# Two window-attention blocks rewritten: 32-row score products, strips of windows, other engine orders and longer loops

## The chip, the cores and the metric

The kernel runs on one core of a Trainium2 chip. The metric is device time in microseconds, the median of the runs. The engines are PE (matmul; its weight loads are listed as PEld), DVE (vector), ACT (scalar, activation tables), POOL (GpSimd) and SP, whose queue issues the DMAs. SBUF is the on-chip memory, PSUM the eight accumulator banks (512 float32 in each of 128 partitions) that PE writes.

## What is computed

The input is float32, 32 images of 56 x 56 tokens of 96 channels. Two transformer blocks follow each other.

```python
# first block ("swin"): 12 heads of 8, windows of 7x7, shifted by 3
xs = jnp.roll(x, (-3, -3), axis=(1, 2)); xw = windows(xs)            # 2048 windows of 49 tokens
q, k, v = heads(xw @ qkv_w + qkv_b)
attn = einsum('whqd,whkd->whqk', q, k) / clip(|q| |k|, 1e-6) / clip(tau, 0.01)
attn = softmax(attn + bias + mask)                                    # bias by a small network
out = roll(unwindow(einsum('whqk,whkd->whqd', attn, v) @ proj_w + proj_b), (3, 3))
x = x + ln(out) * g1 + b1
x = x + ln(gelu(x @ fc1_w + fc1_b) @ fc2_w + fc2_b) * g2 + b2         # hidden layer of 384
# second block ("plain"): 6 heads of 16, windows of 8x8, no shift, norm ahead of each part
x = x + attention(ln(x) * g1 + b1)
x = x + gelu((ln(x) * g2 + b2) @ w_fc1 + b_fc1) @ w_fc2 + b_fc2
```

## The kernel before, in words

`two_blocks` calls `block_program` for each block; the first writes its result to `between_blocks` in DRAM and the second reads it. A block works on groups of 8 windows, four pairs: 256 groups in the first, 196 in the second. Tokens of a pair lie in the partitions (98 or 128), or, transposed, the 96 features do (392 or 512 columns a group).

Each engine runs its own program of the same form: `run_groups` calls `body(g, r)` for each g, with eleven calls written out, a hardware loop `Fori` of four calls to a turn (61 turns in the first block, 46 in the second), and nine more calls. In `body` the stages are staggered: it works on the attention of group g, transposes and projects group g+2 or g+1 (`turn`, `make`), and does projection and MLP of groups g-2 to g-4 (`out2`, `mlp`, `fin`). A body has four slots, one for each pair. The order of all work on an engine is what the source says; semaphores named in `STEPS` order the engines among one another.

For a pair: PE computes scores (L617) into `psS`, half of the output partitions for each window of the pair. The contraction runs over 128 rows: `q_band` holds three copies of the queries, each with only one band of 32 features filled (DVE L963 in the first block, ACT L855 and DVE L999 in the second), and `k_heads` holds the keys spread over heads (POOL L1051, product with a mask). In the first block DVE adds the bias in two halves (L903), takes the greatest score (L907), POOL subtracts it (L1062); in the second DVE does both (L911, L913). ACT takes exponentials (L798). PE turns them (L747) into `psP`, two banks, and ACT copies them (L788). PE multiplies by the values (L691) and, for two pairs, adds up the heads (L699). DVE takes the reciprocal (L1027) and multiplies (L1032) into `mixedT`. Projection (L630), MLP (L580 to L582 for products with a high and a low part, L640 for fc2), transposes (L661, L711), values (L731), and the squared norms of the first block (L719) use `psM` (two banks) and `psT` (one). Scores of a pair run in slot s, their turning one slot later, the values two slots later.

In the first block, a window row's pair is loaded by one DMA or more (`swin_windows`), in rows of 96 channels, and the bottom row of windows has its own order of tokens, so that the bias network is computed for two orders in the set-up (L428, L438).

Of the kernel before, what the change touches and what calls it, by code (L numbers as in the profile page):

```python
# [33 lines left out]
F32 = mybir.dt.float32  # L34
# [16 lines left out]
class Swin:  # L51
# [3 lines left out]
    cosine = True  # L55
    score_banks = 2

    score_parts = [(0, 0, 4, 0, 0), (1, 0, 2, 0, 196), (1, 2, 2, 1, 0), (2, 0, 4, 1, 98)]


class Plain:
# [3 lines left out]
    cosine = False  # L65
    score_banks = 1
    score_parts = [(0, 0, 2, 0, 0), (1, 0, 2, 0, 128), (2, 0, 2, 0, 256)]
# [15 lines left out]
    "q_band0": "first band of the plain block's queries", "q_band": "queries, one copy to a band, other bands zero", "k_hat": "keys ready to be spread over heads",  # L83
    "k_heads": "keys spread over heads, for one pair", "v_made": "values in dense bank 0", "v_heads": "... and in SBUF",
    "scored0": "scores in their first bank", "scored1": "scores in their second bank",
    "score_read0": "first score bank read", "score_read1": "second score bank read",
# [4 lines left out]
    "inv_total": "1 / sum, for two pairs", "mixedT": "two pairs' attention output, feature-major in SBUF",  # L91
    "proj_made": "projection in dense bank 0", "proj_read": "... and read",
    "y_ln": "normalised projection", "y_var": "variance", "y_eps": "+ epsilon", "y_rstd": "power -1/2",
# [49 lines left out]
def block_program(nc, cfg, src, dst, par, const, psum):  # L143

    win, heads, groups = cfg.win, cfg.heads, cfg.groups
# [7 lines left out]
    cosine = cfg.cosine  # L153
    SB = cfg.score_banks
    SBC = SC // SB
# [4 lines left out]

    ctx = ExitStack()
    with ctx:
        def sb(name, shape, dtype=F32):
            return ctx.enter_context(nc.sbuf_tensor(f"{cfg.name}_{name}", shape, dtype))


        did = {name: ctx.enter_context(nc.semaphore(f"{cfg.name}_{name}")) for name in STEPS}
        if not cosine:

            did.update(q_read=did["q_band"], k_read=did["k_hat"], score_read0=did["shifted"],  # L170
                       proj_read=did["x1"], fc2_read=did["x2"])
# [1062 lines left out]
```

## Time and profile before

| | |
|---|---|
| median of 3 runs | 9856.51 us (9837.21 to 9867.02) |
| profiled execution, span | 9836.7 us |
| PE busy | 8863.2 us, 90% |
| DVE busy | 8255.4 us, 84% |
| ACT busy | 6463.2 us, 66% |
| POOL busy | 6006.3 us, 61% |
| granted TensorE clock, mean | 0.969 |

The profiled execution's own time outside the span is not listed; its span lies 20 us under the median. The first block fills roughly the first 6060 us, the second the rest. Busy shares are averages over the two blocks; the stages have to be read apart. One fp32 product is listed as two records.

### The profile page before, as it was taken

The numbers are of one execution on the slowest core, as the hardware profiler recorded it, in microseconds if no ns is written. First come the engines' busy times: TensorE is split into PE (matmuls) and PEld (weight loads), VectorE is DVE, ScalarE is ACT, GpSimd is POOL, SyncE is SP. The second block draws the span as 40 slices with busy tenths as digits, with TensorE's granted clock in tenths as the row PEclk, the third lists the DMA queues.
The fourth block names the chain that finished last, engine by engine and source line by source line (L and its number), as shares of the span: only waits on it lengthen the run. The fifth ranks groups of instructions, "written<-read, shape, count | busy, mean of one in ns | idle before, by whom it ended". The sixth has DMA issues, their size and how long they took to land. (4 is left out here: it accounts for less than half of the span.)

```text
span 9836.7 us, 333424 instructions
## 1 busy us (share of the span) xinstructions
PE 8863.2 (90%) x117550; PEld 6763.6 (69%) x117550; DVE 8255.4 (84%) x16517; ACT 6463.2 (66%) x10305; POOL 6006.3 (61%) x8277
## 2 busy tenths in 40 slices
PE   7888888888888888888888886999999999999999
PEld 5666666666666666666666665777777777777777
DVE  5998898898898898898898896877777777777777
ACT  4666666666666666666666665666666666666666
POOL 4777677676777776777776775544444444444444
PEclk9999999999999999999999998999999999999999
DMA  0000000000000000000000000000000010000010
GB/s 12 15 16 15 15 16 15 15 16 15 15 16 15 16 16 14 16 15 15 16 15 15 16 15 16 22 23 23 23 23 21 23 23 22 22 22 23 23 23 22
DMA packets 465836, 175.87 MB, mean 18 GB/s; under 512 B 463833, under 2 KB 464601, under 8 KB 464601
## 3 DMA queue, kind: packets, MB, share of 16 engines
q1 hardware_dynamic: 464602, 155.98, 7.0%
q8 instruction: 1195, 19.58, 0.9%
q14 instruction: 39, 0.31, 0.0%
HBM read 78.68 MB, written 77.07 MB: 16 GB/s over the span
## 5 line engine op out<-in xcount | busy, mean ns | idle before, releaser
L1062 POOL TENSOR_TENSOR swin_score<-swin_score,swin_top 113x588 f32<-113x588 f32 x1024 | 1269.0, 1239 | 1468.4 <-DVE swin_top L907 1468.4
L788 ACT ACTIVATE swin_probT<-ps_probs 128x678 f32<-128x678 f32 x1024 | 751.4, 734 | 1410.4 <-PE ps_probs L747 1410.1
L617 PE MATMUL ps_scores<-swin_k_heads,swin_q_band 128*64 128x196 f32 (+3 forms) x16384 | 1262.4, 296 | 124.7 <-issue 124.7
L1051 POOL TENSOR_TENSOR swin_k_heads<-swin_k_hat,swin_head_mask 96x196 f32<-96x196 f32 x2048 | 1316.3, 670 | 27.9 <-DVE swin_k_hat L959 27.9
L788 ACT ACTIVATE plain_probT<-ps_probs 128x384 f32<-128x384 f32 x784 | 380.2, 485 | 1142.8 <-PE ps_probs L747 1123.3
L617 PEld LDWEIGHTS ps_scores<-swin_k_heads,swin_q_band 128*49 128x49 f32 (+1 forms) x16384 | 845.6, 131 | 353.8 <-issue 202.6
L1051 POOL TENSOR_TENSOR plain_k_heads<-plain_k_hat,plain_head_mask 96x128 f32<-96x128 f32 x1568 | 578.9, 401 | 797.4 <-ACT plain_k_hat L847 797.4
L903 DVE TENSOR_TENSOR swin_score<-ps_scores,swin_bias_tab 113x294 f32<-113x294 f32 x2048 | 869.7, 454 | 162.3 <-PE ps_scores L617 140.0
L617 PE MATMUL ps_scores<-plain_k_heads,plain_q_band 128*64 128x128 f32 x9408 | 722.4, 291 | 154.1 <-issue 140.5
L798 ACT ACTIVATE swin_prob<-swin_score 113x588 f32<-113x588 f32 x1024 | 720.2, 703 | 190.8 <-POOL swin_score L1062 186.0
L907 DVE TENSOR_REDUCE swin_top<-swin_score 113x12 f32<-113x588 f32 x1024 | 784.4, 766 | 35.1
L747 PE MATMUL ps_probs<-swin_ident,swin_prob 113*128 113x113 f32 x6144 | 793.1, 265 | 1.9 <-ACT swin_prob L798 1.9
L691 PE MATMUL ps_mixed<-swin_probT,swin_v_heads 128*32 128x49 f32 x24576 | 562.2, 209 | 241.8 <-DVE swin_mixedT L1032 241.5
L963 DVE TENSOR_TENSOR swin_q_band<-swin_qk,swin_sq_norm 32x392 f32<-32x392 f32 x768 | 759.8, 989 | 7.0
L617 PEld LDWEIGHTS ps_scores<-plain_k_heads,plain_q_band 128*64 128x64 f32 x9408 | 528.8, 142 | 337.0 <-issue 292.0
L691 PEld LDWEIGHTS ps_mixed<-swin_probT,swin_v_heads 128*32 128x32 f32 x24576 | 422.2, 109 | 463.8 <-DVE swin_mixedT L1032 314.7
L747 PEld LDWEIGHTS ps_probs<-swin_ident,swin_prob 113*128 113x128 f32 x6144 | 645.2, 141 | 136.2 <-issue 90.1
L1027 DVE RECIPROCAL swin_inv_total<-ps_mixed 96x196 f32<-96x196 f32 x512 | 699.6, 1366 | 0.0
L1027 DVE RECIPROCAL plain_inv_total<-ps_mixed 96x256 f32<-96x256 f32 x392 | 679.5, 1734 | 0.2 <-PE ps_mixed L699 0.2
L640 PE MATMUL ps_dense<-plain_w_fc,plain_hid 128*128 128x96 f32 x4704 | 662.1, 306 | 0.8 <-ACT plain_hid L771 0.8
L640 PEld LDWEIGHTS ps_dense<-plain_w_fc,plain_hid 128*128 128x128 f32 x4704 | 646.9, 223 | 1.2 <-ACT plain_hid L771 1.2
L1101 POOL TENSOR_TENSOR plain_var_eps<-plain_moments,plain_epsilon 128x4 f32<-128x4 f32 x196 | 39.0, 199 | 993.4 <-DVE plain_moments L917 993.4
(180 smaller groups left out, 23375.5 us busy)
## 6 DMA issues: line engine op xcount, KB each, us to landing
plain_x_in<-between_blocks SPq DMA_DIRECT2D x784, 48.0 KB, 2.2
out_dram<-plain_x SPq DMA_DIRECT2D x784, 48.0 KB, 2.0
swin_x_in<-in_x SPq DMA_DIRECT2D x672, 36.8 KB
between_blocks<-swin_x SPq DMA_DIRECT2D x672, 36.8 KB
swin_x_in<-in_x SPq DMA_DIRECT2D x448, 7.9 KB
between_blocks<-swin_x SPq DMA_DIRECT2D x448, 7.9 KB
swin_x_in<-in_x SPq DMA_DIRECT2D x224, 28.9 KB
between_blocks<-swin_x SPq DMA_DIRECT2D x224, 28.9 KB
```

The lines of the kernel that those rows point to most:

```text
L617: last = nc.tensor.matmul(psS[half * HALF:half * HALF + rows, bank if SB == 2 else slot % 2, col:col + nj * WIN], q_band[:, r % 2, band, w ...
L640: last = nc.tensor.matmul(psM[0:TT, 1, p * DIM:(p + 1) * DIM], hid[:, c, p * TT:(p + 1) * TT], w_fc2[:, c, :], start=(c == 0), stop=(c == ...
L691: last = nc.tensor.matmul(psO[32 * band:32 * band + 32, first:first + WIN], v_heads[:, at, 2 * as_ + half, band, n, :], turned[:, band * H ...
L747: last = nc.tensor.transpose(psP[:, bank, hp % 3 * QT:(hp % 3 + 1) * QT], prob[0:QT, ts % 2, 2 * hp:2 * hp + 2, :].rearrange("p h k -> p ( ...
L788: nc.scalar.activation(to, frm, ACT.Copy).then_inc(did["probT"], 1)
L798: nc.scalar.activation(prob[0:QT, es % 2, :, 0:WIN], score[0:QT, es % 2, :].rearrange("p (h k) -> p h k", k=WIN), ACT.Exp).then_inc(did["p ...
L903: nc.vector.tensor_tensor(score[0:QT, half, cols], psS[0:QT, bank, 0:SBC], kind.rearrange("p o n -> p (o n)"), ALU.add)\
L907: nc.vector.tensor_reduce(top[0:QT, half, :], heads_view, AX.X, ALU.max).then_inc(did["top"], 1)
L963: last = nc.vector.tensor_tensor(q_band[rows, (r + 1) % 2, band, 0:NT], qk[rows, 0, :], sq_norm[rows, 0, :], ALU.mult)
L1027: nc.vector.reciprocal(inv_total[:, :], psO[0:DIM, SUMS:SUMS + 2 * TT])\
L1051: last = nc.gpsimd.tensor_tensor(k_heads[0:DIM, (r + 1) % 2, w, :].rearrange("c (j k) -> c j k", j=J), bcast(k_hat[:, w * WIN:(w + 1) * WI ...
L1062: nc.gpsimd.tensor_tensor(view, view, bcast(top[0:QT, half, :], 2, WIN), ALU.subtract)\
```

## The change

`block_program` is split into `swin_block` and `plain_block`, each with its own PSUM tensors. `run_groups` gets an `unroll`, 40 groups for a turn in the first block (6 turns) and 36 in the second (5 turns); 16 or more groups stand outside.

Both blocks: scores are computed band by band, each with 32 rows of queries (`q_hat`, one copy) and 32 rows of keys, into one bank a band. `psS` holds one pair (three banks), `psP` is one bank. Part of the reciprocals (all of them in the first block, every second one in the second) is made on ACT as exp(-ln(x)).

First block: a group is a strip of windows. Tile i of a strip holds every fourth column, so that four neighbouring tokens are one row of 1536 bytes in DRAM (`strip`). Features of a head are set apart by 4 (`by_turns`), and the spreading of keys is four DMAs (`spread`) on SP. `psM` has three banks A, B, C, and `psT` is gone. Each pair's exponentials are turned in two halves of three, two slots after the scores, and the values follow three slots after. `x1` is made by DVE out of `y`, the squares of z by POOL. The bias network runs for one order of tokens.

Second block: the values' product moves to slot 3, and the steps of the MLP are in another order.

```diff
-def run_groups(engine, groups, body):
+def run_groups(engine, groups, unroll, body):
     for g in range(-3, 8):
-        body(g, g % 4)
-    with engine.Fori(2, groups // 4 - 1) as m:
-        for r in range(4):
-            body(4 * m + r, r)
-    for g in range(groups - 4, groups + 5):
-        body(g, g % 4)
+        body(g, g % 8)
+    with engine.Fori(0, (groups - 16) // unroll) as m:
+        for k in range(unroll):
+            body(unroll * m + 8 + k, k % 8)
+    for g in range(8 + (groups - 16) // unroll * unroll, groups + 5):
+        body(g, g % 8)
...
-                                        psS[half * HALF:half * HALF + rows, bank if SB == 2 else slot % 2,
-                                                col:col + nj * WIN],
-                                            q_band[:, r % 2, band, w * WIN:w * WIN + rows],
-                                            k_heads[:, r % 2, w, j0 * WIN:(j0 + nj) * WIN], start=True, stop=True)
+                                for band in range(BANDS):
+                                    part = slice(32 * band, 32 * band + 32)
+                                    last = nc.tensor.matmul(psS[half * HALF:half * HALF + rows, band, 0:BC], q_hat[part, r % 2, w * WIN:w * WIN + rows], k_heads[part, r % 2, :, w * WIN:(w + 1) * WIN], start=True, stop=True)
...
+                def spread(n, parity):
+                    sp.wait_ge(did['k_hat'], upto(n))
+                    sp.wait_ge(did['scored'], upto(n - 2, PAIRS - 1, PAIRS))
+                    for j in range(J):
+                        sp.dma_start(k_heads[j:DIM:J, parity, j, :], k_hat[j:DIM:J, :]).then_inc(did['k_spread'], 16)
...
+                    def turn_probs(tg, ts, part):
+                        if exists(tg, groups):
+                            pe.wait_ge(did['prob'], upto(tg, ts, PAIRS))
+                            ug, us = before(tg, ts, 1)
+                            pe.wait_ge(did['probT'], upto(tg, 2 * ts, 2 * PAIRS) if part else upto(ug, 2 * us + 1, 2 * PAIRS))
+                            for n in range(3):
+                                hp = 3 * part + n
+                                last = nc.tensor.transpose(psP[:, n * QT:(n + 1) * QT], prob[0:QT, ts, 2 * hp:2 * hp + 2, :].rearrange('p h k -> p (h k)'), ident[0:QT, 0:QT])
+                            last.then_inc(did['prob_turned'], 1)
...
+                    def invert_totals(mg, ms):
+                        if ms % 2 == 1 and exists(mg, groups):
+                            act.wait_ge(did['mixed_made'], upto(mg, ms, PAIRS))
+                            act.wait_ge(did['mixedT'], upto(mg, ms // 2 - 1, 2) if ms > 1 else upto(mg - 1, 1, 2))
+                            nc.scalar.activation(inv_total[:, :], psO[0:DIM, SUMS:SUMS + 2 * TT], ACT.Ln).then_inc(did['log_total'], 1)
+                            act.wait_ge(did['log_total'], upto(mg, ms // 2, 2))
+                            nc.scalar.activation(inv_total[:, :], inv_total[:, :], ACT.Exp, scale=-1.0).then_inc(did['inv_total'], 1)
...
+                        if slot == 2:
+                            gelu(2)
+                            copy_turned(*before(g, slot, 2), 0)
+                            act.preload_act_table_set(EXP_SET)
+                            exponentials(*before(g, slot, 1))
+                            invert_totals(*before(g, slot, 3))
+                        if slot == 3:
+                            if exists(turn, groups):
+                                act.wait_ge(did['q_read'], upto(turn))
+                                act.wait_ge(did['norms_made'], upto(make))
+                                nc.scalar.activation(qk_sq[:, :, :], qk[:, :, :], ACT.Square).then_inc(did['qk_sq'], 1)
+                            copy_turned(*before(g, slot, 2), 0)
```

## Rows read from the trace of the kernel before

**Rows 1.** The stretches table: us; busy us (x instructions) of each engine; granted clock; DMA.
```profile
3000.00:4000.00 1000.00, 881.36 (x12876) 670.70 (x12877) 895.52 (x1552) 661.10 (x1035) 704.34 (x863) 0.99 0.07 15
...
8000.00:9000.00 1000.00, 956.17 (x10789) 734.71 (x10788) 775.54 (x1928) 658.68 (x1092) 480.85 (x834) 0.93 0.10 22
```

**Rows 2.** PE's timeline in the first block: start us, us, what; pause before, releaser.
```profile
4000.62 0.93 PE L630 MATMUL ps_dense<-swin_w_proj,swin_mixedT 97*98 97x96 f32 x8
...
4004.77 1.22 PE L617 MATMUL ps_scores<-swin_k_heads,swin_q_band 128*64 128x196 f32 x16
4005.91 0.45 PE L580 MATMUL ps_dense<-swin_x1T_high,swin_w_fc_high 96*128 96x392 f32 x1
...
4014.38 0.55 PE L691 MATMUL ps_mixed<-swin_probT,swin_v_heads 128*32 128x49 f32 x24 [0.92 <-DVE swin_mixedT L1032]
...
4017.11 0.84 PE L699 MATMUL ps_mixed<-swin_probT,swin_sum_heads 128*32 128x196 f32 x12
4018.82 0.54 PE L711 MATMUL ps_turn<-swin_ident,swin_x 98*96 98x98 f32 x4 [0.87 <-POOL swin_x L1118]
...
4022.93 0.93 PE L630 MATMUL ps_dense<-swin_w_proj,swin_mixedT 97*98 97x96 f32 x8
```

**Rows 3.** PE's timeline in the second block.
```profile
8013.70 0.88 PE L617 MATMUL ps_scores<-plain_k_heads,plain_q_band 128*64 128x128 f32 x12
8014.51 1.13 PE L630 MATMUL ps_dense<-plain_w_proj,plain_mixedT 96*128 96x96 f32 x8
8015.48 2.84 PE L640 MATMUL ps_dense<-plain_w_fc,plain_hid 128*128 128x96 f32 x24
...
8030.97 0.88 PE L617 MATMUL ps_scores<-plain_k_heads,plain_q_band 128*64 128x128 f32 x12
```

**Rows 4.** Groups of POOL's instructions by line, 500 to 5500 us: count, busy, mean ns, idle before.
```profile
L1051 POOL TENSOR_TENSOR swin_k_heads<-swin_k_hat,swin_head_mask 96x196 f32<-96x196 f32 x1730 | 1112.2, 671 | 12.6 <-DVE swin_k_hat L959 12.6
L1062 POOL TENSOR_TENSOR swin_score<-swin_score,swin_top 113x588 f32<-113x588 f32 x866 | 1074.0, 1240 | 1240.4 <-DVE swin_top L907 1240.4
```

**Rows 5.** The same view of the second block, 6300 to 9600 us.
```profile
L1077 POOL TENSOR_TENSOR plain_x_res<-plain_x_in,plain_res_row 128x384 f32<-128x384 f32 x172 | 171.4, 996 | 0.0
```

**Rows 6.** PE's timeline in the first block, at the end of a loop body.
```profile
4068.56 1.44 PE L617 MATMUL ps_scores<-swin_k_heads,swin_q_band 128*64 128x196 f32 x16 [2.01 <-issue]
```

**Rows 7.** PE's timeline in the second block, at the end of a loop body.
```profile
8051.12 0.88 PE L617 MATMUL ps_scores<-plain_k_heads,plain_q_band 128*64 128x128 f32 x12 [2.97 <-issue]
...
8053.01 5.33 PE L640 MATMUL ps_dense<-plain_w_fc,plain_hid 128*128 128x96 f32 x24
```

**Rows 8.** The stretches table, four microseconds behind that stall.
```profile
8055.00:8059.00 4.00, 4.00 (x29) 3.66 (x29) 0.44 (x1) 0.00 (x0) 0.00 (x0) 0.50 0.23 49
```

**Rows 9.** Groups of DVE's instructions by line and shape, 3000 to 5000 us.
```profile
L903 DVE TENSOR_TENSOR swin_score<-ps_scores,swin_bias_tab 113x294 f32<-113x294 f32 x693 | 294.4, 454 | 55.4 <-PE ps_scores L617 47.2 <-issue 4.9
...
L963 DVE TENSOR_TENSOR swin_q_band<-swin_qk,swin_sq_norm 32x392 f32<-32x392 f32 x259 | 256.9, 992 | 2.4
L1027 DVE RECIPROCAL swin_inv_total<-ps_mixed 96x196 f32<-96x196 f32 x173 | 236.4, 1366 | 0.0
```

**Rows 10.** Groups of ACT's instructions by line and shape, 3000 to 5000 us.
```profile
L788 ACT ACTIVATE swin_probT<-ps_probs 128x678 f32<-128x678 f32 x346 | 253.9, 734 | 481.8 <-PE ps_probs L747 481.8
...
L831 ACT ACTIVATE swin_z_sq<-swin_z 98x384 f32<-98x384 f32 x86 | 45.0, 524 | 0.0
```

**Rows 11.** SP's timeline of DMA issues, 4000 to 4040 us.
```profile
4006.70 4.97 SPq L521 DMA_DIRECT2D swin_x_in<-in_x  x5
```

**Rows 12.** The page's part 6: DMA issues, count, KB each, us to landing.
```profile
plain_x_in<-between_blocks SPq DMA_DIRECT2D x784, 48.0 KB, 2.2
```

**Rows 13.** Groups by line and shape in the second block, 7000 to 9000 us.
```profile
L1027 DVE RECIPROCAL plain_inv_total<-ps_mixed 96x256 f32<-96x256 f32 x209 | 362.2, 1733 | 0.0
```

**Rows 14.** The whole timeline of the set-up.
```profile
32.17 16.68 PE L438 MATMUL ps_scores<-meta_w,meta_hidden 96*49 96x12 f32 x196 [0.35 <-ACT meta_hidden L465]
...
62.89 16.67 PE L438 MATMUL ps_scores<-meta_w,meta_hidden 96*49 96x12 f32 x196 [0.35 <-ACT meta_hidden L465]
```

More of the change, by code:

```diff
@@ L82 @@
     "sq_norm": "squared norms with their floor in SBUF", "log_norm": "their logarithm", "inv_norm": "1 / norm",
[L83 to L86, printed above, removed]
+    "reciprocal": "1 / sum of a group's last two pairs in the second block",
+    "k_heads": "a pair's keys spread over heads",
+    "q_hat": "queries ready for the scores", "k_hat": "keys ready to be spread over heads",
+    "k_spread": "a head's keys of every band are in their own columns", "v_made": "values in dense bank 0", "v_heads": "... and in SBUF",
+    "scored": "a pair's scores in psS, one bank to a band", "score_read": "... and read",
     "top": "greatest score of each query and head", "shifted": "scores less their top",
@@ L163, in sb @@
         def sb(name, shape, dtype=F32):
[L164 to L171, printed above, removed]
+            return ctx.enter_context(nc.sbuf_tensor(f'{cfg.name}_{name}', shape, dtype))
@@ L323, in block_program @@
+            for band in range(BANDS):
+                for j in range(J):
+                    first = 32 * band + j * D
+                    loads += [(b_qk[32 * band + j:32 * band + 32:J, t:t + 1], column(par['qkv_b'][t * DIM + first:t * DIM + first + D])) for t in range(2)]
             with nc.Block() as block:
@@ new lines, in _ @@
+                @block.scalar
+                def _(act):
+                    act.wait_ge(s_par, 16 * len(loads))
+                    cols = WIN * WIN
+                    for n, a in enumerate(range(0, cols, 480)):
+                        b = min(a + 480, cols)
+                        act.wait_ge(did['setup_hidden'], n + 1)
+                        nc.scalar.activation(hidden[:, a:b], psM[0:DIM, 1, 0:b - a], ACT.Relu, bias=meta_b1[:, :]).then_inc(s_act, 1)
+        PLAIN_ROW, LAST_ROW = (3, 11)
@@ new lines, in store @@
+                def store(n, parity):
+                    sp.wait_ge(did['x2'], upto(n))
+                    for p in range(PAIRS):
+                        rows, cols = place(n, p)
+                        sp.dma_start(dst_rows[rows, cols, :], x2[:, parity, p, :]).then_inc(s_store[parity], 16)
+                for n in range(8):
+                    load(n, n % 2)
+                with sp.Fori(4, groups // 2) as m:
+                    for k in range(2):
+                        load(2 * m + k, k)
+                        store(2 * m + k - 8, k)
@@ L563, in _ @@
+                for n in range(groups - 8, groups):
+                    store(n, n % 2)
                 for parity in range(2):
@@ new lines, in body @@
+                    exponentials(2)
+                    if exists(make, groups):
+                        act.wait_ge(did['k_made'], upto(make))
+                        act.wait_ge(did['k_heads'], upto(g, PAIRS - 1, PAIRS))
+                        nc.scalar.activation(k_hat[:, :], psM[0:DIM, B, 0:NT], ACT.Identity, bias=b_qk[:, 1:2]).then_inc(did['k_hat'], 1)
+                    if exists(turn, groups):
+                        nc.scalar.activation(xT_high[:, r % 2, :], psT[0:DIM, 0:NT], ACT.Copy).then_inc(did['xT'], 1)
@@ L892, in body, with shift @@
+                def body(g, phase):
+                    r = phase % 4
+                    turn, make, out1, out2, mlp, fin = (g + 2, g + 1, g - 1, g - 2, g - 3, g - 4)
+                    def shift(slot):
                         if exists(g, groups):
```

1769 lines of the change are left out of this document (969 added, 800 removed).

## The prediction

> **What bounds the kernel now.** I read the table of stretches first. In the first block DVE is busy 896 of 1000 us and PE 881; in the second PE is busy 956 and DVE 776 [rows 1]. So the first block has two nearly full engines, the second has one. Next I read PE's timeline for the time of one group. In the first block a group takes 4022.93 - 4000.62 = 22.3 us. In it PE stands 0.92 us for `mixedT` of DVE and 0.87 us for `x1` of POOL [rows 2]; with a third, smaller pause some 20.1 us are work. In the second block a group takes 8030.97 - 8013.70 = 17.3 us [rows 3] with hardly any pause: PE alone sets it.
>
> These are not the averages. The first block makes 866 shifts, 216.5 groups, in 5000 us: 23.1 us a group [rows 4]. The second makes 172 groups in 3300 us: 19.1 us [rows 5]. The difference is met once in four groups, at the end of the loop body: PE stands 2.01 us before `ps_scores` in the first block [rows 6] and 2.97 us in the second [rows 7], both "issue", that is, waiting for no other engine. Behind the second one the granted clock is 0.50 for 4 us [rows 8], its lower level, 1.2 GHz, and the MLP's last products take 5.33 us there [rows 7]. So a turn of the loop costs 4 x (23.1 - 22.3) = 3.1 us in the first block and 4 x (19.1 - 17.27) = 7.4 us in the second.
>
> **Long loops.** The first block's loop turned 61 times and will turn 6 times, the second's 46 and 5 times. If each turn keeps its price, this saves 55 x 3.1 = 170 us and 41 x 7.4 = 303 us. Nothing else is hidden behind these stalls. The bounds: nothing is saved if the code of a long body stalls by itself, 473 us if only the turn does. Inside the four groups of a body, and in the unrolled groups around the loop, I found no such stall, so I take the upper one. SP keeps its loop of eight groups in the first block.
>
> **Scores in strips of 32 rows.** Before, a pair's scores stream 588 columns in sequence for each window (both windows beside each other on two halves of the output) and take 4005.91 - 4004.77 = 1.14 us; in the second block 384 columns take 8014.51 - 8013.70 = 0.81 us [rows 2, 3]. That is 0.33 us for 204 columns, 1.62 ns each, and 0.19 us that doesn't scale. Afterwards each of three bands uses its own 32 rows of the array and its own bank, 196 (128) columns each. If the bands run beside one another: 0.19 + 0.32 = 0.51 us in the first block, 0.19 + 0.21 = 0.40 in the second. If they don't, 588 (384) columns are left and nothing changes. The trace shows no products on different rows side by side. It does show it for different output columns: the sums over heads, on strips of 32 output columns, pass 12 x 196 = 2352 columns in 0.84 us [rows 2], 2.8 columns a ns, more than the 2.4 cycles a ns that the upper level of the clock has. I take the lower value, as a column strip and a row strip are alike cut out of the array, and keep the other end as a rival. Saved: 4 x 0.63 = 2.5 us and 4 x 0.41 = 1.6 us of PE in each group. A rule speaks for less: the Trainium skill, "TensorE: Matmul & The Clock Gate", Part 3: Packing small matmuls, measured 2.38 times for three strips and 6.32 times for nine, some 70 to 79% of full concurrency; an estimate by it is 0.13 us more for each pair, 0.5 us a group, some 200 us in the sum. No run here shows it yet.
>
> **First block, the other engines.** Busy shares times 23.1 us give DVE 20.7, ACT 15.3 and POOL 16.3 us a group [rows 1].
> - DVE: three `q_band` copies of 0.99 us become one product over as many columns: -2.0. Two reciprocals of 1.37 us go: -2.7. Two additions of 0.45 us for a pair become one; a start costs some 0.15 of each, so -0.6 for four pairs [rows 9]. A read of `proj` with the gain comes in: +0.5. The four steps of `y_ln` stay as steps that make `x1`. Left: 15.9.
> - POOL: eight spreadings of the keys at 0.67 us go, and the addition of `x1`, 384 columns, at about 1.0; the squares of z come, as many columns at the same price [rows 4, 5]. Left: 10.9.
> - ACT: four copies of 678 columns at 0.73 us become eight of 339; by the line through 678 and 384 columns (0.52 us) one is 0.49 [rows 10]: +1.0. Squares of z go (-0.5), the copy `y` goes (about -0.5). Two logarithms and two exponentials of 196 columns come, at 0.3 to 0.4 us each: +1.3. Left: 16.6.
> - PE: 20.1 - 2.5 = 17.6, and 0.2 for turns cut in halves.
>
> No engine is full at 17.8, but they are chained. `psP` is now one bank that is filled twice for each pair, and ACT must empty it before PE goes on. ACT does so in a fixed order among its other steps. I laid the steps of one group in order, with the durations above, each starting at the later of its engine and its inputs. Slots 0 and 1 run at PE's speed, to 5.3 and 10.6 us. In slot 2 ACT has gelu(2), a copy, a table load, the exponentials and then the inverse of the sums, which is ready at 15.2 us. DVE's `mixedT` waits for it, and behind it on DVE are queued the reads of queries and keys, done at 16.7; then come ACT's squares (17.6), its next copy out of `psP` (18.0), PE's next turn and PE's norms at 19.8 us. So slot 3 has some 2 us of PE waiting, and the group takes 19.8 us. This wait takes the place of the two that were there. Gain: 256 x (22.32 - 19.8) = 645 us. The bounds are 17.8 (all hidden) and 22.3 (the chain is as long as the old group).
>
> **Key spread by DMA.** POOL's spreading becomes four transfers on SP's queue. SP now issues 3 loads, 4 spreads and 3 stores a group, where it had 5 and 5, at 0.99 us each [rows 11]. Transfers of plain rows land 2.2 us after their issue [rows 12]. `k_hat` is ready 8.4 us into a group, the spread keys are wanted at 19.8: 11.4 us, against 4 + 2.2 = 6.2. I cost it at nothing; the rest of the group hides it. On SP the spread stands behind a load that waits for `x_res` of POOL (about 4.7 us into the group) and takes 3 us to issue, done at 7.7; behind the spread stands a store, which has eight groups of room. Without the cover, each microsecond beyond 11.4 costs 256 us. Longer rows in DRAM (1536 bytes instead of 384) can only make loads shorter, and no load is waited for in the steady state.
>
> **Second block.** PE -1.6 us for the scores. Two `q_band` steps of ACT and DVE's one merge into one DVE step, one of two reciprocals of 1.73 us goes to ACT as two steps of about 0.4 [rows 13]. Those engines had room. `psS` and `psP` lose their second buffer: scores of a pair now wait until the pair before is shifted, and a turn until the copy of the one before. In my ordering of the steps DVE shifts a pair 1.5 to 2 us before PE wants the bank, and ACT empties `psP` at least 0.3 us before, with one wait of 0.15 us in slot 2. So the group is 17.27 - 1.64 = 15.63. Gain: 196 x 1.64 = 321 us. The bounds of the group are 15.6 (nothing waits) and 17.27 (all of it is lost to the single buffers).
>
> **Set-up.** The bias network is computed once, not for two orders: the second pass starts 62.89 - 32.17 = 30.7 us after the first [rows 14]. Twenty-two more small loads come; at no more than 0.99 us each [rows 11] they cost up to 22, and I take 10, as they move far less. Saved: 20 us, nothing of it hidden.
>
> **Sum.** 645 + 170 + 321 + 303 + 20 = 1459 us. The profiled span is 9836.7 us, so 8378 us. The median of the runs stands 20 us over that span (9856.5), so 8398, given as 8400 us.
>
> **Rivals.**
> - The chain in the first block is fully hidden and PE sets the group at 17.8 us: 8400 - 256 x 2.0 = 7890 us. For it: the queues of the engines are ordered anew, and DVE and POOL get lighter. Against it: the ordered walk above. Chance 0.2.
> - The chain through the single `psP` bank leaves the first block's group at 22.3 us although no engine is full: 8400 + 645 = 9045 us. For it: two more round trips between PE and ACT per pair, each with its hand-over. Chance 0.15, with the way there.
> - The change doesn't do what it says: 32-row products run one after another. Then PE has 20.3 us of work in the first block, with the chain about 21.8 us, and 17.27 in the second: 8400 + 256 x 2.0 + 321 = 9233 us. Chance 0.07. The Trainium skill, "TensorEngine Tiling (Array Packing)", Gotcha 1: PSUM Pressure, asks for different banks for different rows, which this code gives; by it this rival is unlikely.
> - Long bodies stall as often as short ones: 8400 + 473 = 8873 us. Chance 0.05.
> - Slower: PE's clock. The products of fc2 take 5.33 us at the lower level against 2.84 us otherwise [rows 3, 7], 1.88 times. PE's work after the change is 256 x 17.8 + 196 x 15.6 = 7610 us; if the lower level holds for a share s of it, 0.88 x 7610 x s is added. From s = 0.22 the gain of 1459 is gone. With the whole first block at the lower level: 8400 + 256 x (17.8 x 1.88 - 19.8) = 11900 us. Against it: the granted clock was 0.99 [rows 1] with PE standing still for 1.8 us of each 22.3. For it: PE will stand longer in slot 3, and smaller strips are lighter work. Chance 0.03.
>
> **How the numbers follow.** The forecast has a chance of 0.5; the likeliest time is 8400 us. The range is 7900 to 8950 us: it takes in full hiding (0.2), the stalling bodies (0.05) and the way to the old group length, and leaves out that length itself, one-after-another strips and the clock, together some 0.2. A measurement of this kernel can tell some 0.3%, 30 us, from no change. Only the clock rival is slower: faster 0.96, same 0.01, slower 0.03.
>
> **What would show it.** In the changed kernel's table of stretches, POOL near 55% and PE near 90% in the first block. PE's timeline: scores in 0.5 and 0.4 us, a stall at "issue" only every 40 or 36 groups, a group of 19.8 and 15.6 us. The waits: PE for ACT's copy of turned exponentials, and `norms` for the squares. Wrong would be a wait of `scores` for the spread keys, scores of over 0.8 us, or a granted clock under 0.9 over a whole stage.

## The result

The changed kernel takes 8816.67 us (median of four runs, 8814.72 to 8822.26) against 9848.81 us before; the ratio is 0.8957, with a 95% interval of 0.8937 to 0.8977. The forecast was 8400 us with a range of 7900 to 8950 us. So the sign and the range were right, and 427 of the 1459 us of gain did not come.

The page of the changed kernel: busy us, share of the span and instructions of each engine; then the granted clock in 40 slices.

```profile
PE 7940.9 (90%) x113246; PEld 5701.5 (65%) x113246; DVE 7158.3 (81%) x14526; ACT 6444.2 (73%) x11835; POOL 4747.7 (54%) x6229
...
PEclk9999999999999999999999999799999999999999
```

Its table of stretches, one in each block (columns as in [rows 1]):

```profile
3000.00:4000.00 1000.00, 877.23 (x13191) 620.37 (x13188) 849.50 (x1357) 740.22 (x1401) 541.42 (x561) 0.96 0.09 23
7000.00:8000.00 1000.00, 976.27 (x12956) 717.51 (x12955) 798.90 (x2260) 745.23 (x1315) 563.97 (x1000) 0.99 0.12 27
```

POOL is at 54% and PE at 88% in the first block, as forecast. But the granted clock is 0.96 there, where it was 0.99 [rows 1]; in the second block it is 0.99, where it was 0.93 [rows 1]; the run with long loops alone, below, shows why.

Where the time went is read from three marks on PE's timeline: the first turn of an input (L661 before, L533 and L1098 after) and the last fc2 (L640 before, L526 after). First the kernel before, then the changed one:

```profile
89.48 0.89 PE L661 MATMUL ps_turn<-swin_ident,swin_x_in 98*96 98x98 f32 x4 [9.93 <-DMA swin_x_in<-in_x]
...
6026.74 4.31 PE L640 MATMUL ps_dense<-swin_w_fc,swin_hid 128*98 128x96 f32 x24 [0.68 <-ACT swin_hid L771]
...
6079.56 1.09 PE L661 MATMUL ps_turn<-plain_ident,plain_x_norm 128*96 128x128 f32 x4 [9.46 <-POOL plain_x_norm L1071]
```

```profile
69.78 0.89 PE L533 MATMUL swin_ps_dense<-swin_ident,swin_x_in 98*96 98x98 f32 x4 [8.37 <-DMA swin_x_in<-in_x]
...
5588.37 2.32 PE L526 MATMUL swin_ps_dense<-swin_w_fc,swin_hid 128*98 128x96 f32 x24 [0.68 <-ACT swin_hid L594]
...
5632.05 1.09 PE L1098 MATMUL plain_ps_turn<-plain_ident,plain_x_norm 128*96 128x128 f32 x4 [9.44 <-POOL plain_x_norm L1335]
```

| stretch | before | after | gained | forecast |
|---|---|---|---|---|
| set-up | 89.5 | 69.8 | 20 | 20 |
| first block | 5941.6 | 5520.9 | 421 | 645 + 170 |
| between the blocks | 48.5 | 41.4 | 7 | 0 |
| second block, to the end of the span | 3757.1 | 3188.4 | 569 | 321 + 303 |

(The spans are 9836.7 and 8820.4 us.) The first block holds 394 us of the shortfall. Here is one of its groups in PE's timeline, from its projection to the next one, with slot 3 in between:

```profile
3036.19 0.90 PE L500 MATMUL swin_ps_dense<-swin_w_proj,swin_mixedT 97*98 97x96 f32 x8 [1.02 <-issue]
...
3051.31 0.51 PE L478 MATMUL swin_ps_probs<-swin_ident,swin_prob 113*128 113x113 f32 x3 [0.24 <-ACT swin_probT L603]
...
3053.66 0.51 PE L478 MATMUL swin_ps_probs<-swin_ident,swin_prob 113*128 113x113 f32 x3 [1.36 <-ACT swin_probT L603]
3054.01 1.48 PE L562 MATMUL swin_ps_dense<-swin_qk_sq,swin_same_head 96*96 96x392 f32 x4
3055.42 0.56 PE L492 MATMUL swin_ps_scores<-swin_k_heads,swin_q_hat 32*64 32x196 f32 x12
3057.00 0.90 PE L500 MATMUL swin_ps_dense<-swin_w_proj,swin_mixedT 97*98 97x96 f32 x8 [1.02 <-issue]
```

and what the other engines do there:

```profile
3051.23 1.15 DVE L731 TENSOR_SCALAR swin_qk<-swin_ps_dense,swin_b_qk 96x392 f32<-96x392 f32 x2
...
3052.41 0.86 ACT L650 ACTIVATE swin_qk_sq<-swin_qk 96x784 f32<-96x784 f32 x1 [1.15 <-DVE swin_qk L731]
...
3053.17 0.43 ACT L603 ACTIVATE swin_probT<-swin_ps_probs 128x339 f32<-128x339 f32 x1
...
3053.77 2.65 DVE L737 SCALAR_TENSOR_TENSOR swin_z_ln<-swin_z,swin_z_rstd,swin_gain 98x96 f32<-98x96 f32 x4
...
3053.93 1.18 POOL L760 TENSOR_TENSOR swin_score<-swin_score,swin_top 113x588 f32<-113x588 f32 x1 [1.79 <-DVE swin_top L683]
...
3055.07 1.00 POOL L792 TENSOR_TENSOR swin_x_res<-swin_x,swin_res_row 98x384 f32<-98x384 f32 x1
...
3056.35 0.55 DVE L741 TENSOR_TENSOR swin_x1T_low<-swin_ps_dense,swin_x1T_high 96x392 fp32r<-96x392 f32 x1
```

Read it in this order. ACT takes the squares (L650) before its copy out of `psP` (L603), and the squares wait 1.15 us for DVE's reads of queries and keys. So PE stands 1.36 us. Then the projection (L500) stands 1.02 us; "issue" means that the profile names no releaser, but the code has it wait for `x1T_low`, which starts on DVE at 3056.35, the moment that four `z_ln` steps of 2.65 us in sum are done. Beside them POOL works nearly all the time, with its shift and its residual. A group without disturbance takes 20.81 us (3057.00 - 3036.19, from projection to projection), not 19.8. And the average between 2000 and 4000 us is 21.40 us, since the granted clock falls to its lower level, 1.2 GHz, behind every fourth slot 3 or so (23 falls in these 2000 us, 157 us together at the lower level; 21 of the 23 begin within 1 us of the end of the 1.36 us pause). The row in the middle of this table of stretches is such a place:

```profile
2990.00:3008.00 18.00, 16.55 (x256) 11.82 (x254) 15.38 (x25) 13.80 (x27) 10.59 (x12) 1.00 0.10 27
3011.00:3017.00 6.00, 6.00 (x59) 3.67 (x60) 5.10 (x8) 2.36 (x5) 2.74 (x4) 0.50 0.00 0
3018.00:3032.00 14.00, 13.12 (x216) 9.75 (x214) 11.30 (x19) 10.67 (x22) 7.11 (x8) 1.00 0.13 35
```

### The profile page after: what moved, and what is told of

Same layout as the page of the kernel before. It is cut to its first block and busy times, and to the rows that moved or that the text cites. A ratio compares the mean times of both kernels' runs of the same rounds, so it can differ in the third digit from the quotient of the medians.

```text
span 8820.4 us, 316771 instructions
## 1 busy us (share of the span) xinstructions
PE 7940.9 (90%) x113246; PEld 5701.5 (65%) x113246; DVE 7158.3 (81%) x14526; ACT 6444.2 (73%) x11835; POOL 4747.7 (54%) x6229
## 5 line engine op out<-in xcount | busy, mean ns | idle before, releaser
L603 ACT ACTIVATE swin_probT<-swin_ps_probs 128x339 f32<-128x339 f32 x2048 | 911.1, 445 | 1020.0 <-PE swin_ps_probs L478 1015.0
L478 PE MATMUL swin_ps_probs<-swin_ident,swin_prob 113*128 113x113 f32 x6144 | 982.2, 269 | 413.0 <-ACT swin_probT L603 412.5
L478 PEld LDWEIGHTS swin_ps_probs<-swin_ident,swin_prob 113*128 113x128 f32 x6144 | 724.4, 144 | 553.3 <-ACT swin_probT L603 466.2
L681 DVE TENSOR_TENSOR swin_score<-swin_ps_scores,swin_bias_tab 113x588 f32<-113x588 f32 x1024 | 780.8, 762 | 123.0 <-PE swin_ps_scores L492 115.2
L737 DVE SCALAR_TENSOR_TENSOR swin_z_ln<-swin_z,swin_z_rstd,swin_gain 98x96 f32<-98x96 f32 x1024 | 673.9, 717 | 4.2 <-POOL swin_z_rstd L788 4.2
L526 PEld LDWEIGHTS swin_ps_dense<-swin_w_fc,swin_hid 128*98 128x98 f32 x6144 | 557.6, 168 | 94.5 <-issue 93.5
L492 PE MATMUL swin_ps_scores<-swin_k_heads,swin_q_hat 32*64 32x196 f32 (+1 forms) x12288 | 599.9, 359 | 12.8 <-issue 11.7
L526 PE MATMUL swin_ps_dense<-swin_w_fc,swin_hid 128*98 128x96 f32 x6144 | 599.4, 254 | 0.7 <-ACT swin_hid L594 0.7
L460 PE MATMUL swin_ps_mixed<-swin_probT,swin_v_heads 128*32 128x49 f32 x24576 | 583.6, 214 | 0.6 <-ACT swin_probT L603 0.6
L1077 PE MATMUL plain_ps_dense<-plain_w_fc,plain_hid 128*128 128x96 f32 x4704 | 569.6, 279 | 0.8 <-ACT plain_hid L1151 0.8
```

The lines of the kernel that those rows point to most:

```text
L460: last = nc.tensor.matmul(psO[32 * band:32 * band + 32, first:first + WIN], v_heads[:, at, 2 * as_ + half, band, n, :], probT[:, as_, band ...
L478: last = nc.tensor.transpose(psP[:, n * QT:(n + 1) * QT], prob[0:QT, ts, 2 * hp:2 * hp + 2, :].rearrange('p h k -> p (h k)'), ident[0:QT, ...
L492: last = nc.tensor.matmul(psS[half * HALF:half * HALF + rows, band, 0:BC], q_hat[part, r % 2, w * WIN:w * WIN + rows], k_heads[part, r % 2 ...
L526: last = nc.tensor.matmul(psM[0:TT, B, p * DIM:(p + 1) * DIM], hid[:, c, p * TT:(p + 1) * TT], w_fc2[:, c, :], start=c == 0, stop=c == CHU ...
L603: nc.scalar.activation(to, psP[:, 0:3 * QT], ACT.Copy).then_inc(did['probT'], 1)
L681: nc.vector.tensor_tensor(score[0:QT, half, :].rearrange('p (b n) -> p b n', b=BANDS), psS[0:QT, :, 0:BC], kind, ALU.add).then_inc(did['sc ...
```

## The experiments

The runs were made in four sets, each with runs of the kernel before: its median was 9849 us in the set of the result and 9831 (e1 to e4), 9822 (e5 to e8) and 9827 us (e9 to e12) in the others. A comparison across sets is therefore uncertain by some 25 us, and group times from the traces decide where that matters. "Group" below is the time between two projections of the first block on PE's timeline: first its undisturbed value, then the mean between 2000 and 4000 us. A "fall" is a change of the granted clock to its lower level, counted in the same 2000 us.

**Loop length alone (e1_before_long).** The kernel before, with `run_groups` as in the changed kernel:

```
-    with engine.Fori(2, groups // 4 - 1) as m:
-        for r in range(4):
-            body(4 * m + r, r)
+    with engine.Fori(0, (groups - 16) // unroll) as m:   # 40, 36
+        for k in range(unroll):
+            body(unroll * m + 8 + k, k % 4)
```

> The kernel before with nothing changed but the length of the loop bodies: 40 groups in the first block (6 turns) and 36 in the second (5 turns). By the forecast a turn keeps its price of 3.1 and 7.4 us: 55 x 3.1 + 41 x 7.4 = 473 us less, 9376 us. By the trace of the changed kernel a turn of a long body costs about 5.2 and 12 us; then 6 x 5.2 + 5 x 12 = 91 us are left of 530, 439 us less, 9410 us. If long bodies stall inside as often as short ones turn: 9849 us. If the second block's lower granted clock before (0.93) was an effect of its turns, the clock of that stretch should rise to about 0.99.

Measured: 9372.27 us, ratio 0.9538 (0.9521 to 0.9555). The marks on PE's timeline are

```profile
5854.94 4.32 PE L641 MATMUL ps_dense<-swin_w_fc,swin_hid 128*98 128x96 f32 x24 [0.68 <-ACT swin_hid L772]
...
5908.59 1.09 PE L662 MATMUL ps_turn<-plain_ident,plain_x_norm 128*96 128x128 f32 x4 [9.45 <-POOL plain_x_norm L1072]
```

with a span of 9371.6 us and the first turn of an input at 89.59. The first block lost 172 us (forecast 170), the second 294 (303). So long bodies do not stall inside, and the loop term was right to 2%. The granted clock of the second block, 7000 to 8000 us, is 0.99 here and 0.94 in the kernel before: its lower value belonged to the turns, as the expectation had it. What the new bodies added is then the rest of the table: 421 - 172 = 249 us in the first block (forecast 645) and 569 - 294 = 275 us in the second (321).

**Short loops under the new bodies (e2_after_short).** `run_groups(..., 8, body)` and `(..., 4, body)` for 40 and 36.

> The changed kernel with bodies of 8 groups in the first block (30 turns for 6) and of 4 in the second (45 for 5). At the turn prices of the kernel before: 24 x 3.1 + 40 x 7.4 = 370 us more, 9187 us. At the prices seen in the changed kernel (5.2 and 12 us): 24 x 5.2 + 40 x 12 = 605 us more, 9422 us; that would hold if a turn is dear because of the new bodies and not because of their length.

Measured: 9049.18 us, ratio 0.9204 (0.9182 to 0.9226), some 232 us more. Both expectations were too high. The undisturbed groups are unchanged (20.81 and 15.75 us). In the trace of the changed kernel the loop goes back to its start 5 times in the first block, for 3.8 us each, and 4 times in the second, for 11.3 us each: 64 us. So the 73 returns here cost (232 + 64) / 73 = 4.1 us each. The high price of a turn in the second block is not a property of the new bodies: in e1 too, with the old bodies in loops of 36 groups, a return costs 10 us there.

**Two theories for the first block.** Theory D: DVE's string of steps, from `mixedT` to `z_ln` and `x1T_low`, sets the group. Rival P: the single bank `psP` sets it, through ACT's copies. Two edits of order tell them apart.

**ACT's copy first (e3_copy_first).**

```
 if slot == 3:
+    copy_turned(*before(g, slot, 2), 0)
     if exists(turn, groups):
         ... ACT.Square ... 'qk_sq'
-    copy_turned(*before(g, slot, 2), 0)
```

> The changed kernel; in slot 3 of the first block ACT empties the bank of turned exponentials ahead of the squares of queries and keys, so that PE's turn no longer waits 1.36 us for that copy. Theory D (DVE's string of steps from mixedT to z_ln and x1T_low, 6 us without an idle moment, sets the group): the wait moves to the projection behind it, the group stays 20.8 us, 8817 us within 0.5%. Rival P (the single bank psP sets the group, as the prediction had it): the norms start 0.6 us earlier and the group is 20.2 us: 256 x 0.6 = 154 us less, 8663 us.

Measured: 9426.36 us, ratio 0.9592 (0.9574 to 0.961), 610 us slower than the changed kernel. Neither theory had this. PE's timeline:

```profile
3014.51 0.51 PE L478 MATMUL swin_ps_probs<-swin_ident,swin_prob 113*128 113x113 f32 x3
3015.47 1.56 PE L562 MATMUL swin_ps_dense<-swin_qk_sq,swin_same_head 96*96 96x392 f32 x4 [0.44 <-ACT swin_qk_sq L651]
3016.95 0.56 PE L492 MATMUL swin_ps_scores<-swin_k_heads,swin_q_hat 32*64 32x196 f32 x12
3019.14 1.62 PE L500 MATMUL swin_ps_dense<-swin_w_proj,swin_mixedT 97*98 97x96 f32 x8 [1.63 <-issue]
```

and the stretches around it:

```profile
3013.00:3019.00 6.00, 3.76 (x49) 1.79 (x47) 5.87 (x11) 3.73 (x8) 3.35 (x4) 0.99 0.01 2
3019.00:3025.00 6.00, 5.86 (x57) 4.73 (x58) 2.93 (x5) 3.02 (x6) 3.08 (x3) 0.50 0.01 3
3026.00:3036.00 10.00, 9.94 (x166) 7.43 (x170) 8.65 (x13) 8.39 (x15) 5.15 (x5) 1.00 0.12 28
```

The wait for the copy is gone and the wait for `x1T_low` has grown by 0.6 us, as theory D said. But now PE is busy only 3.76 of 6 us, and right behind that the clock falls, in nearly every group (83 falls in 83 groups). The projection takes 1.62 us instead of 0.90. The typical group is 23.89 us, the mean 23.81. Only one of these groups is free of the lower level, and it takes 20.80 us: theory D's value, not rival P's 20.2.

**x1T_low ahead of z_ln (e4_low_first).**

```
 if slot == 3:
+    ... 'x1T_low'
     ... four z_ln steps
-    ... 'x1T_low'
     ... 'sq_norm'
```

> The changed kernel; in slot 3 of the first block DVE makes x1T_low ahead of the four z_ln steps (2.65 us). Theory D: the projection of the next group no longer stands 1.02 us, and the group is 19.8 us: 256 x 1.0 = 256 us less, 8560 us; half of it if sq_norm, now 0.4 us later, is waited for. Rival P (the psP bank sets the group): PE is free 1.0 us earlier but stands for its turns instead, 8817 us within 0.5%.

Measured: 9091.12 us, ratio 0.9254 (0.9237 to 0.9271), 274 us slower. PE's timeline:

```profile
3003.09 0.51 PE L478 MATMUL swin_ps_probs<-swin_ident,swin_prob 113*128 113x113 f32 x3 [0.24 <-ACT swin_probT L603]
...
3005.44 0.51 PE L478 MATMUL swin_ps_probs<-swin_ident,swin_prob 113*128 113x113 f32 x3 [1.36 <-ACT swin_probT L603]
...
3007.69 0.93 PE L500 MATMUL swin_ps_dense<-swin_w_proj,swin_mixedT 97*98 97x96 f32 x8
...
3022.84 0.51 PE L478 MATMUL swin_ps_probs<-swin_ident,swin_prob 113*128 113x113 f32 x3 [0.24 <-ACT swin_probT L603]
```

The projection's pause is gone. From one first turn of slot 3 to the next, a stretch in which the clock holds, it is 3022.84 - 3003.09 = 19.75 us, as theory D said. But the clock now falls 54 times in 2000 us, for 551 us together, and no group from projection to projection is free of it: the shortest is 21.64 us, the mean 22.65. The row of the fall that follows:

```profile
3015.00:3025.00 10.00, 8.41 (x145) 5.90 (x144) 9.34 (x16) 8.37 (x17) 6.20 (x7) 1.00 0.16 45
3025.00:3035.00 10.00, 9.81 (x74) 6.20 (x75) 6.03 (x10) 5.22 (x11) 5.22 (x5) 0.51 0.01 2
```

The two together led to a new theory, G: what both edits lose is PE's granted clock behind the pauses of slot 3. It says that filling a pause with work for PE should give back all of it. The rival says that the order of the steps itself costs the time.

**The same, with the pause filled (e5_low_first_filled).**

```
+if slot == 3 and exists(turn, groups):
+    pe.wait_ge(did['k_read'], upto(turn))
+    nc.tensor.matmul(psM[0:DIM, B, 0:392], same_head[:, :], qk[:, 1, 0:392], start=True, stop=True)
+    nc.tensor.matmul(psM[0:DIM, B, 0:160], same_head[:, :], qk[:, 1, 0:160], start=True, stop=True)
 if slot == 3:
     turn_probs(*before(g, slot, 2), 1)
```

> The kernel of the run with x1T_low ahead of z_ln, and in slot 3, where PE stands 1.36 us for ACT's copy of turned exponentials, two products whose result is never read (392 and 160 columns, some 1.0 us, written to a dense bank that the norms overwrite). Theory G (the lost time is PE's granted clock, which falls behind the pauses of slot 3): the clock of the first block stays near 1.00 and each group takes the 19.8 us that undisturbed groups took there: 8817 - 256 x (21.35 - 19.8) = 8420 us. Rival (the order of DVE's steps itself costs the time, through the later sq_norm): the added products cost or change nothing, 9090 us.

Measured: 8409.56 us, ratio 0.8565 (0.8551 to 0.858). Two products that nobody reads make the kernel 680 us faster. The stretch:

```profile
3000.00:4000.00 1000.00, 962.22 (x14449) 677.80 (x14447) 893.75 (x1462) 797.34 (x1510) 583.47 (x604) 1.00 0.09 25
```

The group is 19.75 us, mean 19.86, with two falls in 2000 us. The added products leave the undisturbed time as it was, so it is the clock that they give back. The order of the steps was right and the clock had hidden it. (The kernel of e3 was not run with its pause filled.)

**Both orders (e6_low_and_copy_first) and both filled (e8_both_filled).** The edits of e3 and e4 together; e8 adds one product of 192 columns ahead of the norms.

> Both edits of order together (x1T_low ahead of z_ln, ACT's copy ahead of the squares), no added products. Each alone cost time at a lower granted clock. Together PE has only 0.24 and 0.44 us of pauses left. Theory G, by pauses: short pauses leave the clock at its upper level, the group is 19.1 to 19.8 us, 8250 to 8420 us. Rival, by order (each edit costs 270 and 610 us against the changed kernel, whatever the pauses): the costs add, 9700 us.

> Both edits of order, and one product of 192 columns whose result is never read where PE stands 0.44 us before the norms. Theory G: the clock of the first block stays near 1.00, the group is 19.1 to 19.8 us: 8250 to 8420 us. If the run without the product already keeps the clock, the two are the same within 0.3%.

Measured: 8345.07 us (ratio 0.8502, 0.8488 to 0.8516) and 8318.66 us (0.8476, 0.8462 to 0.849). The undisturbed group is 19.17 us in both, the mean 19.59 and 19.48, with 9 and 6 falls. Two edits that cost 610 and 274 us alone gain about 470 us together: the costs do not add. PE's pauses in slot 3 are then 0.24 and 0.44 us, and in e8 0.25 us alone.

In both kernels there is a new wait, which the changed kernel does not have. In e8's list of PE's waits, 2000 to 4000 us (us in all, times, longest):

```profile
PE swin_ps_scores L492 <- DMA swin_k_heads<-swin_k_hat: 15.2, 13, 1.7
```

Once in eight groups, the length of SP's loop, scores wait for the spread keys; over the first block 30 waits, 37 us. In e5, with groups of 19.75 us, there are 11 such waits and 4 us. So with these orders of steps, at 19.2 us a group, the key spread is no longer hidden.

**z_ln early (e7_zln_early).** The four `z_ln` steps moved to the head of slot 3, ahead of the addition of the bias.

> The changed kernel with DVE's four z_ln steps at the head of slot 3, ahead of the addition of the bias, where POOL stands still. If POOL's work beside them makes them slow (2.65 us for four, against 1.2 us in the kernel before), they take 1.2 to 1.4 us here; if they are slow by themselves, 2.65 us again. The projection's pause of 1.02 us should go either way. PE still stands 1.36 us in slot 3 as in the run with x1T_low first, so by theory G the clock falls about as there: about 9090 us. If the clock holds, 19.8 us a group, 8420 us.

Measured: 9106.46 us, ratio 0.927 (0.9253 to 0.9287), clock 0.87 in the first block, 53 falls: theory G's price. The four steps take 4 x 0.308 = 1.23 us, as expected if POOL's work beside them is what makes them slow. The groups of DVE's instructions, 3000 to 4000 us, in the kernel before, the changed one and this one (count, busy us, mean ns):

```profile
L1019 DVE SCALAR_TENSOR_TENSOR swin_z_ln<-swin_z,swin_z_rstd,swin_gain 98x96 f32<-98x96 f32 x173 | 50.7, 349 | 0.0
```
```profile
L737 DVE SCALAR_TENSOR_TENSOR swin_z_ln<-swin_z,swin_z_rstd,swin_gain 98x96 f32<-98x96 f32 x188 | 124.8, 723 | 0.0
```
```profile
L678 DVE SCALAR_TENSOR_TENSOR swin_z_ln<-swin_z,swin_z_rstd,swin_gain 98x96 f32<-98x96 f32 x178 | 44.2, 308 | 0.0
```

The same instruction takes 308 ns where POOL stands still and 723 ns on average in the changed kernel. Its single steps there are either fast or very slow; the four of one group (count: least, median and greatest ns):

```profile
L737 DVE SCALAR_TENSOR_TENSOR swin_z_ln<-swin_z,swin_z_rstd,swin_gain x4: 305/680/1229, 3033.0 to 3035.3; 98x96 f32<-98x96 f32 x4
```

They take 310, 1229, 1049 and 305 ns. The last begins when POOL's two steps are over. Between 3000 and 4000 us no `z_ln` step with POOL idle beside it takes more than 307 ns here (47 steps), and none more than 313 ns in e7 (178 steps); the 141 with POOL at work take 862 ns on average. The Trainium skill, "SBUF — State Buffer", section "SBUF: two separate sides", says that a DVE operation with two inputs in SBUF and a POOL operation that reads SBUF share a pair of ports, and that whoever comes second is blocked until the other has finished. The trace agrees: `z`, the gain and the scores that POOL shifts all lie in SBUF, and the two slow steps last about as long as POOL's (1.18 and 1.00 us).

**The changed order, filled (e9_after_filled).** The two products of e5 in the changed kernel itself.

> The changed kernel in its own order, and in slot 3 of the first block the two products of 392 and 160 columns whose result is never read, where PE stands for ACT's copy. This parts the clock's share of the loss from that of the order of steps. Theory G+D: the granted clock rises from 0.96 to 1.00 and each group takes the undisturbed 20.81 us, no less, because DVE's string still ends it: 256 x 0.44 = 112 us less, 8705 us. If the whole loss was the clock: 19.8 us a group, 8420 us. If the added products are themselves in the way: 8817 us or more.

Measured: 8672.2 us, ratio 0.8825 (0.881 to 0.8839). The clock is 1.00, there is one fall in 2000 us, and the group is 20.81 us, mean 20.85. So of the first block's shortfall the clock is 256 x (21.40 - 20.85) = 141 us and the order, with the slow `z_ln`, 256 x (20.81 - 19.8) = 259 us, together 400 us for the 394 us that are missing.

**Scores twice (e10_scores_twice).** `for half in (0, 1, 0, 1)` in the second block's scores.

> The changed kernel; in the second block, where PE alone sets the group, each pair's scores are issued twice (the same products to the same places). This prices the 32-row products in place. If the three bands run beside one another, a pair costs the 0.39 us between its start and that of the next work: 4 x 196 x 0.39 = 306 us more, 9120 us. If the bands ran one after another (0.81 us, as the full-row products before): 635 us more, 9450 us.

Measured: 8943.06 us, ratio 0.9102 (0.9086 to 0.9117), some 126 us more. First the changed kernel, then this one:

```profile
7004.06 0.46 PE L1029 MATMUL plain_ps_scores<-plain_k_heads,plain_q_hat 32*64 32x128 f32 x12
7004.45 0.50 PE L1011 MATMUL plain_ps_dense<-plain_x1T_high,plain_w_fc_high 96*128 96x512 f32 x1
```
```profile
7002.24 0.68 PE L1029 MATMUL plain_ps_scores<-plain_k_heads,plain_q_hat 32*64 32x128 f32 x24
7002.85 0.50 PE L1011 MATMUL plain_ps_dense<-plain_x1T_high,plain_w_fc_high 96*128 96x512 f32 x1
```

From start to start it is 0.39 and 0.61 us. The second half costs 0.22, not 0.39: the rest does not scale, as the prediction had split it (0.19 fixed, 0.21 for the columns). I had priced the experiment as if nothing were fixed. The group is 16.41 us for 15.75, three times 0.22; one of the four falls into the 0.24 us in which PE waits for ACT anyway.

**Longer loops (e11_longer_loops) and all with early z_ln (e12_all_with_early_z_ln).** e11 is e8 with 120 and 60 groups a body. e12 is e8 with e7's place of `z_ln` instead of e4's.

> The kernel with both edits of order and the filled pause, with bodies of 120 groups in the first block (2 turns for 6) and 60 in the second (3 turns for 5). With 5.2 us a turn in the first and some 10 in the second: 4 x 5.2 + 2 x 10 = 41 us less, 8278 us. If a turn's price grows with the length of its body, or long bodies stall inside: no gain or a loss, 8319 us or more.

> ACT's copy ahead of the squares, the filled pause, and z_ln at the head of slot 3 in place of x1T_low ahead of z_ln. DVE's work falls by 1.2 us a group, as z_ln runs without POOL beside it. If DVE still sets the group (19.17 us with both edits), it falls to 18.4 us or so: 256 x 0.75 = 190 us less, 8130 us. If PE and the hand-overs with ACT now set it, DVE's time is worth nothing: 8319 us within 0.5%. If the shift of slot 3, now 1 us later, is waited for, up to 256 us more.

Measured: 8278.16 us (ratio 0.8423, 0.8409 to 0.8437) and 8265.4 us (0.8409, 0.8395 to 0.8423). e11 gives the 41 us, 6.8 us for each of the six turns saved, though as a comparison across sets that is only a little more than its uncertainty. e12 takes DVE from 923 to 857 busy us in 1000, yet the undisturbed group stays at 19.15 us: DVE no longer sets it. The 53 us come from the mean group (19.26 for 19.48, 0.22 x 256 = 56 us), and most of that is the key spread: no scores wait for it in e12, which is worth the 37 us of e8. The clock falls 2 times and not 6, 14 us at the lower level for 24 us, which is the smaller part. e12 is the fastest kernel run, 6.1% below the changed one by the ratios. It was not run with e11's loops.

## Why the prediction was right and where it was wrong

- **Long loops**, 473 us: right; 466 by e1 (172 and 294). A slip in the working did no harm: 3300 / 172 is 19.19 us a group, which gives 7.7 us a turn and not 7.4. The assumption that a turn keeps its price was not quite right either, but few turns are left. e2's short bodies give 4.1 us a turn; in the changed kernel a turn of the second block costs up to 12 us. PE's timeline shows two pauses there, and the stretch behind them the lower clock:

```profile
6927.91 0.46 PE L1029 MATMUL plain_ps_scores<-plain_k_heads,plain_q_hat 32*64 32x128 f32 x12 [2.97 <-issue]
...
6931.00 1.99 PE L1070 MATMUL plain_ps_dense<-plain_w_proj,plain_mixedT 96*128 96x96 f32 x8 [2.62 <-issue]
```
```profile
6930.00:6935.00 5.00, 4.00 (x19) 4.03 (x20) 1.97 (x4) 1.81 (x2) 2.60 (x3) 0.50 0.03 7
```

- **Scores in strips**, 0.51 and 0.40 us: right. They take 0.39 us in the second block (above) and 0.49 in the first (start to start in the changed kernel, the two rows below). The rival that they run one after another is out. The 0.13 us more for a pair, an estimate from the figures of the Trainium skill, "TensorE: Matmul & The Clock Gate", Part 3: Packing small matmuls, did not show: the first block's 0.49 us is below the 0.51 without it.

```profile
3020.20 0.56 PE L492 MATMUL swin_ps_scores<-swin_k_heads,swin_q_hat 32*64 32x196 f32 x12
3020.69 0.45 PE L443 MATMUL swin_ps_dense<-swin_x1T_high,swin_w_fc_high 96*128 96x392 f32 x1
```

- **Second block's group**, 15.63 us: right, 15.75. The single buffers cost one wait of 0.24 us where 0.15 was forecast. 275 of 321 us came: 24 us are that 0.12 us a group. Of the other 22 us, the start of the block accounts for most: to its third projection it takes 83.5 us for e1's 72.1, although its groups are shorter; why stays open. The four returns of the loop take some 5 us (11.3 us each for 10.0 in e1).
- **Set-up**, 20 us: right, 19.7.
- **Key spread at nothing**: right for the changed kernel; the list of PE's waits in the first block has none for it. It does not hold for the faster ones: in e6, e8 and e11, at 19.2 us a group, it costs 36 to 37 us. In e12, with the same length of the group, nothing waits for it again: between 2000 and 4000 us SP issues the latest spread 5.1 us behind its `k_hat` there, in e8 7.3 us. Which step of SP's queue makes the difference was not tested.
- **POOL and ACT**: 10.9 and 16.6 us a group forecast; 0.541 x 21.4 = 11.6 and 0.740 x 21.4 = 15.8 measured. **DVE** was forecast at 15.9 and is 0.850 x 21.4 = 18.2. The missing 2.3 us are mostly `z_ln`: 4 x (0.72 - 0.35) = 1.5 us. The new form of `k_hat`, with the temperature in it, takes 1.30 us for 0.84, and `q_hat` 1.18 for the 0.99 taken; together 2.2 us.
- **First block's group**, 22.32 to 19.8 us: this is the step that failed. The walk through the ordered steps got slot 3's wait right (ACT's copy behind the squares, 1.36 and 0.24 us for "some 2 us"), but it stopped at the norms. Behind them DVE's queue goes on: `z_ln`, which the walk took at its old price, then `x1T_low`, for which the next projection waits. With `x1T_low` moved ahead the undisturbed group was 19.75 us, the walk's 19.8. So the walk missed one wait of 1.02 us, 259 us in the sum. The term that it had too small is `z_ln`: at the 0.35 us of the kernel before, the four steps would end some 1.2 us earlier, more than the wait that they cause. No run has this order with `z_ln` at that price; e9 shows the wait without the clock's share, and e4 with e5 that it goes when `x1T_low` does not stand behind the four.
- **The clock**: it stood among the rivals as a rare case that would make the kernel slower, with a chance of 0.03, and at nothing in the sum. It cost 141 us in the changed kernel, and in two kernels that differ from it by one moved step 256 x (mean - undisturbed group) = 770 (e3) and 740 us (e4); e5 gave 682 of e4's back. That the clock was 0.99 with 1.8 us of pauses a group [rows 1, 2] was no ground for leaving it out. Those two pauses, of 0.92 and 0.87 us, begin work again 4.4 us apart, while the changed kernel has one of 1.36 us in slot 3 and others 2.3 us ahead and 3.3 us behind; whether this is what made the difference was not tested.
- **The range**: that it held the result is in part luck. Its upper half stood for long bodies that stall and for a chain through `psP` that comes near the old group. Neither came. What the measured time has above 8400 us comes from DVE's `z_ln` and the clock, and the clock's rival had been left outside the range.

## What to carry to other kernels

Where PE is the fullest engine, look for where its pauses stand, not only for their sum: here one pause of 1.4 to 1.6 us in a group went with a fall of the granted clock, in one group of four (the changed kernel) up to every one (e3), and an edit that shortened the chain cost more than it gained. Before such an edit is given up, fill the pause with a product that nobody reads; if the time falls, it was the clock. And walk the queue of every engine through to the first step of the next group, with the prices that the steps have beside their new neighbours. When the group has become shorter, look again at what was hidden, as the key spread was here.

## What was not expected of the hardware

- The granted clock is very sensitive to order. Pauses of 0.24, 1.36 and 1.02 us a group brought 23 falls in 2000 us; 0.24 and 1.36 us, less in all, brought 54, with 551 us at the lower level; 0.24 and 0.44 us brought 9. Why the smaller sum of e4 fell more often than the larger of the changed kernel stays open: the runs show only that most falls begin behind the 1.36 us pause (21 of 23, and 35 of 54 in e4) and that filling it ends nearly all of them in both. The Trainium skill, "TensorE: Matmul & The Clock Gate", section "A second HAM failure mode: psum-queue depth-cycling", describes such a swing through short idle times between groups of products, with the median product at the full clock. The traces agree: in e4, but for the returns of the loop, PE's pauses are 0.24 and 1.36 us, and the mean clock is 0.86.
- A group of products at the lower level takes nearly twice as long: the projection 1.62 us for 0.90.
- DVE's `z_ln` takes 2.3 times as long on average in the changed kernel as where POOL stands still (723 ns for 308), and a single step up to four times (1229 ns).
- A turn of the loop costs some 4 us with short bodies (e2), 3.8 us with 40 groups in the first block and 11 us with 36 in the second (the changed kernel). The second block's code is the same in e8, e9 and the changed kernel, and yet a turn costs 6 to 9, 4 to 11 and 10 to 12 us there; why stays open.
